# Two-layer graph network: the factor scores of layer 1's loop on GpSimd instead of VectorE

## The chip, the cores and the metric

The kernel runs on one core of a Trainium2 chip. The metric is device time in microseconds (us) of one execution; several executions are taken and their median is given. Engines: TensorE (PE, its weight loads PEld), VectorE (DVE), ScalarE (ACT), GpSimd (POOL) and the DMA queues.

## The reference

Two layers over 2708 nodes with 128 features and a 0/1 adjacency matrix. Layer 0 is a normalised diffusion plus a cosine-similarity attention, with a residual and a layer norm. The change is in layer 1:

```python
XW = jnp.matmul(X, W)
s_col = jnp.matmul(XW, a[0, :f])
s_row = jnp.matmul(XW, a[0, f:])
Z1 = jax.nn.leaky_relu(s_row[:, None] + s_col[None, :], negative_slope=0.01)
den = jnp.exp(Z1)
num = jnp.matmul(A, den)
att = jnp.where(num != 0, den / jnp.where(num != 0, num, 1.0), 0.0)
H = jnp.matmul(A, jnp.matmul(att, XW))
x = _layernorm(x + H)
```

## The kernel before, in words

Nodes are cut into 22 tiles of 128 (T = 22, the last one short). For layer 1 the kernel first ranks all nodes by s_col and by s_row. With columns in that order, the leaky relu of a tile of 128 columns has its kink only in a short window of rows; every row outside the window is on one known side, where exp(s_row + s_col) is a product of two factors. So `num` for a tile jt is a matrix product over few rows: one or two sets of 128 gathered rows of the adjacency (WN = 2; `win` holds the kind: 0 for one set, 1 for two, 2 for a window too wide for this), and a table of sums for all the rest. `FIRST = 4` separates tiles whose window data come early from the others.

The left operands of these products ("factors") lie in `den_w`, `den_h`: for each tile three slots of 128x128 fp32, in a ring of two tiles (DS = 3). A slot is filled in three steps. First the scores: for the window sets q = 0 and, in kind 1, q = 1, `max(s_col + Rw, slope part + r01w)` in the form (column block + per-partition value) max (per-partition value), and for the table slot (column block + e_bias) min e_cap. Second ScalarE's exponential (`den_exp_small`, L718 and L720, one 128x256 instruction, and one more 128x128 in kind 1). Third the low halves: the rest of the fp32 value over its upper bfloat16, computed for the window sets on GpSimd (`halves`, L492 in kind 1, L496 in kind 0) and for the table slot on VectorE (`sums_half`, L1261). TensorE waits for both (`s_denb`) before it sums tile jt.

The loop of layer 1 runs over v = 0..65, three steps v (two blocks of 452 columns each) to a tile. TensorE: `num(v)` (gathered rows L1708, table L1716), then `xw_product(v - 3)` (L1768). ScalarE: two logarithms of the sums (L731), `attention_exp(v - 1)` (L709), and at v = 3(jt-1) + 1 `den_exp_small(jt)`. VectorE: `attention_scores(v)` (L1322), `attention_low(v - 1)` (L1329), at the first step of a tile `small_scores(jt + 1, True)` (L1228 for the window sets, L1247 for the table), at the second `sums_half(jt + 1)`. GpSimd runs by tiles, in order: `fetch_rows(jt)` (two indirect DMAs, L463), `halves(jt - 1)`, `fetch_xw(jt + 4)` (one indirect DMA, L454, up to jt = 17), `split_xw(jt)` (a cast L472 and a subtraction L474 of 128x128).

Each engine carries out its own list in order; semaphores order the engines. `s_num` counts finished sums (6 to a tile), `s_denz` scores (3 to a tile), `s_dene` exponentials, `s_denb` low halves. There is a second form of the loop for inputs with wide windows (`general`); the inputs here take the first.

Of the kernel before, what the change touches and what calls it, by code (L numbers as in the profile page):

```python
# [7 lines left out]
T = 22  # L8
# [19 lines left out]
DS = WN + 1  # L28
# [11 lines left out]
ALU = mybir.AluOpType  # L40
# [42 lines left out]
def rows_of(t):  # L83
    return P if t < T - 1 else LAST


def adj_resnorm2_kernel(nc, x, adjT, alpha, beta, W, a, rowk, out):
    with ExitStack() as ctx:
        def sb(name, shape, dt=F32):
            return ctx.enter_context(nc.sbuf_tensor(name, shape, dt))  # L90

        def sem(name):
            return ctx.enter_context(nc.semaphore(name))
# [27 lines left out]
        tab_part, is_u, e_cap, slot0, no_node = (kc[:, q:q + 1] for q in range(5))  # L121
        own_tile = kc[:, 5:5 + T]
        win = sb("win", [1, 2 * T + 1], I32)
# [34 lines left out]
        e_bias = FR[:, 3356:3356 + T]  # L158
        Rw = FR[:, 3378:3378 + WN * T].rearrange("p (q t) -> p q t", q=WN)
        r01w = FR[:, 3422:3422 + WN * T].rearrange("p (q t) -> p q t", q=WN)  # L160
# [23 lines left out]
        den_w = R1[:, DEN0:DEN0 + NDEN * P].rearrange("p (t j) -> p t j", t=NDEN)  # L184
# [7 lines left out]
        cb3 = cb.rearrange("p (t j) -> p t j", t=T)  # L192
# [55 lines left out]
        s_cball, s_cbc, s_mask, s_count, s_win, s_tabs, s_pick, s_ebias, s_tabh, s_tab = (  # L248
            sem(n) for n in ("s_cball", "s_cbc", "s_mask", "s_count", "s_win", "s_tabs", "s_pick", "s_ebias",
                             "s_tabh", "s_tab"))  # L250
        s_denz, s_dene, s_denb = sem("s_denz"), sem("s_dene"), sem("s_denb")
        s_num, s_ln, s_sub, s_att1, s_alo, s_y, s_xws = (
            sem(n) for n in ("s_num", "s_ln", "s_sub", "s_att1", "s_alo", "s_y", "s_xws"))
# [14 lines left out]
        V, S, G, TE = nc.vector, nc.scalar, nc.gpsimd, nc.tensor  # L268
# [47 lines left out]
        FIRST = 4  # L316
# [37 lines left out]
        def _(eng):  # L354
            gp = Waiting(eng)
# [50 lines left out]
            met = gp.covered()  # L406
# [15 lines left out]
            for it in range(T):  # L422
                m, s = rows_of(it), it % 2
# [29 lines left out]
            def fetch_xw(t):  # L453
                G.indirect_dma_start(out=XWs[:, t, :], out_offset=None, in_=XWd,  # L454
                                     in_offset=bass.IndirectOffsetOnAxis(ap=idx[:, 1, t:t + 1], axis=0)
                                     ).then_inc(s_AT[t], 16)

            def fetch_rows(jt):
                gp.wait_ge(s_idxw, 1 if jt < FIRST else 2)
                if jt >= 3:  # L460
                    gp.wait_ge(s_num, 6 * (jt - 2))
                for q in range(WN):
                    G.indirect_dma_start(out=AW2[:, jt % 3, q, :], out_offset=None, in_=ATd,  # L463
                                         in_offset=bass.IndirectOffsetOnAxis(ap=idxw[:, q, jt:jt + 1], axis=0)
                                         ).then_inc(s_AW[jt % 3], 16)

            def split_xw(t):

                gp.wait_ge(s_AT[t], 32)
                if t >= 4:  # L470
                    gp.wait_ge(s_y, 3 * (t - 3))
                G.tensor_copy(XW2[:, t % 4, 1, :], XWs[:, t, :]).then_inc(s_xws, 1)  # L472
                gp.wait_ge(s_xws, 2 * t + 1)
                G.tensor_tensor(XW2[:, t % 4, 0, :], XWs[:, t, :], XW2[:, t % 4, 1, :], ALU.subtract).then_inc(s_xws, 1)  # L474
# [10 lines left out]
            def halves(jt):  # L485

                s = T + jt % 2 * DS
                kind = eng.value_load(win[0:1, jt:jt + 1], min_val=0, max_val=2)
                gp.wait_ge(s_dene, jt + 1)
                met = gp.covered()  # L490
                with eng.If(kind == 1):
                    G.tensor_tensor(den_h[:, s + 1:s + DS, :, 0], den_w[:, s + 1:s + DS, :], den_h[:, s + 1:s + DS, :, 1],  # L492
                                    ALU.subtract).then_inc(s_denb, 1)
                gp.only(met)
                with eng.Else():
                    G.tensor_tensor(den_h[:, s + 1, :, 0], den_w[:, s + 1, :], den_h[:, s + 1, :, 1], ALU.subtract).then_inc(s_denb, 1)  # L496
                gp.only(met)

            def layer1(general):

                for jt in range(2, T):
                    fetch_rows(jt)
                    if not general:
                        halves(jt - 1)
                    if jt + 4 < T:
                        fetch_xw(jt + 4)
                    split_xw(jt)
                if not general:
                    halves(T - 1)

# [2 lines left out]
            met = gp.covered()  # L513
# [255 lines left out]
        def _(eng):  # L769
# [166 lines left out]
            met, steps = dv.covered(), own.n  # L936
# [145 lines left out]
            for it in range(T):  # L1082
                m, s = rows_of(it), it % 2
# [141 lines left out]
            def score(jt, q):  # L1225

                s = T + jt % 2 * DS
                return V.tensor_scalar(den_w[:, s + 1 + q, :], cb3[:, jt, :], Rw[:, q, jt:jt + 1], r01w[:, q, jt:jt + 1],  # L1228
                                       ALU.add, ALU.max)

            def small_scores(jt, usual):

                s = T + jt % 2 * DS
                if jt >= 2:
                    dv.wait_ge(s_num, 6 * (jt - 1))
                dv.wait_ge(s_pick, 2 if jt < FIRST else 4)
                if usual:
                    kinds[jt] = eng.value_load(win[0:1, jt:jt + 1], min_val=0, max_val=2)
                    met = dv.covered()
                    with eng.If(kinds[jt] == 1):  # L1240
                        score(jt, 1)
                    dv.only(met)
                    score(jt, 0).then_inc(s_denz, 2)
                else:
                    for q in range(WN):
                        score(jt, q).then_inc(s_denz, 1)
                V.tensor_scalar(den_w[:, s, :], cb3[:, jt, :], e_bias[:, jt:jt + 1], e_cap, ALU.add, ALU.min).then_inc(s_denz, 1)  # L1247
# [16 lines left out]
            def den_scores(jt):  # L1264

                dv.wait_ge(s_win, WIN)
                dv.wait_ge(s_pick, 2 if jt < FIRST else 4)
                dv.wait_ge(s_ebias, 1)
                dv.wait_ge(s_cbc, 6)
                where["wide"] = eng.value_load(win[0:1, T + jt:T + jt + 1], min_val=0, max_val=1)  # L1270
                met = dv.covered()
                with eng.If(where["wide"] == 0):
                    small_scores(jt, False)
                dv.only(met)
# [39 lines left out]
            def attention_scores(v):  # L1314

                c0, w = wide_of(v)
                dv.wait_ge(s_negc, 1)
                dv.wait_ge(s_rbm, 6)
                dv.wait_ge(s_ln, 2 * v + 2)
                if v >= NZ:  # L1320
                    dv.wait_ge(s_y, v - NZ + 1)
                V.scalar_tensor_tensor(z_of(v), rb[:, c0:c0 + w], negc[:, v // 3:v // 3 + 1], tL[v % 2][:, 0:w],  # L1322
                                       ALU.max, ALU.subtract).then_inc(s_sub, 1)

            def attention_low(v):

                high, lower = halves_of(v)
                dv.wait_ge(s_att1, v + 1)
                V.tensor_tensor(lower, z_of(v), high, ALU.subtract).then_inc(s_alo, 1)  # L1329

            def layer1(general):

                for v in range(NV):
                    jt, cp = v // 3, v % 3
                    attention_scores(v)
                    if v:
                        attention_low(v - 1)
                    if jt + 1 < T:
                        if general:
                            if cp == 0:  # L1340
                                den_scores(jt + 1)
                            if cp == 1:
                                den_halves(jt + 1)
                            if cp == 2:
                                den_all(jt + 1)
                        else:
                            if cp == 0:
                                small_scores(jt + 1, True)
                            if cp == 1:
                                sums_half(jt + 1)  # L1350
                    if v == 0:
                        table(3)
                        window_rows(FIRST, T, 4)
                    if v == 1:
                        table(4)
                        table(5)
                attention_low(NV - 1)
# [3 lines left out]
            met, steps = dv.covered(), own.n  # L1361
# [499 lines left out]
```

## Time and profile before

| | |
|---|---|
| median of 3 runs | 676.37 us (675.48 to 677.48) |
| profiled execution | 675.03 us |
| its span in the profile | 673.3 us |
| busy over the span: PE, DVE, ACT, POOL | 569.4, 544.2, 352.8, 435.7 us |
| granted TensorE clock, mean | 0.944 |

The span is what the rows below cover; 1.7 us of the profiled execution lie around it. Times are in us from the start of the span unless marked ns. Busy shares are averages over stages that differ much. An instruction's line (L1708) is that of the kernel's text. Layer 1's loop runs from about 393 to 591 us.

### The profile page before, as it was taken

Reading aid. Unit: us, or ns where it says so; the run is one execution under the profiler, and the core shown is the slowest. Engines: PE = TensorE matmul, PEld = TensorE weight load, DVE = VectorE, ACT = ScalarE, POOL = GpSimd, SP = SyncE. Lnnn points to the kernel's source line nnn. Section 1 sums busy time; section 2 is a strip of 40 time slices with the busy share of each in tenths; the row PEclk is TensorE's granted clock in tenths of the full one; section 3 lists DMA queues with packets and bytes.
Section 4 is the critical chain, followed back from the end, with each engine's and each line's share of the span. In section 5 each row is a group of like instructions: output and inputs, shape, how many; then the busy total and the mean of one; then the engine's idle time right before and its main releaser. Section 6 shows DMA issues by size and latency. Waiting matters only on the chain.

```text
span 673.3 us, 11277 instructions
## 1 busy us (share of the span) xinstructions
PE 569.4 (85%) x4123; PEld 348.4 (52%) x4123; DVE 544.2 (81%) x965; ACT 352.8 (52%) x568; POOL 435.7 (65%) x448
## 2 busy tenths in 40 slices
PE   0489999999998679999718988898989999949993
PEld 0245555455453368888617644344445444427883
DVE  1679999999999973678888766899898999985442
ACT  2334544444443542579986226787777788811000
POOL 5849999999998933556305043687786788203663
PEclk9999999999999589999757989999999999988997
DMA  9999891000000000000000041323242333000000
GB/s 148 101 108 108 108 380 51 0 1 1 1 1 1 5 1 17 18 24 17 18 1 21 5 125 46 77 82 103 63 110 72 91 95 98 21 5 13 29 28 18
DMA packets 17797, 37.21 MB, mean 55 GB/s; under 512 B 2570, under 2 KB 8222, under 8 KB 17726
## 3 DMA queue, kind: packets, MB, share of 16 engines
q0 software_dynamic: 7392, 24.32, 20.2%
q1 hardware_dynamic: 10334, 11.98, 5.4%
q8 instruction: 39, 0.64, 0.4%
q14 instruction: 32, 0.26, 0.1%
HBM read 48.72 MB, written 10.45 MB: 88 GB/s over the span
## 4 chain that ended last, share of the span: by engine, by line
PE 35%; POOL 25%; DVE 22%; issue 7%; ACT 7%; DMA 2%; DVEq 0%; POOLq 0%; ACTq 0%; SPq 0%
POOL R L401 23%; PE PSALL L1809 8%; PE PSALL L1708 5%; PE PSALL L1515 5%; DVE ring L1329 4%; DVE ring L1322 4%; ACT AW L629 4%; PE PSALL L1637 3%; PE PSALL L1768 3%; PE PSALL L1441 2%; DVE FR L1329 2%; DVE FR L1322 1%; PE PSALL L1716 1%; PE PSALL L1538 1%; DMA X<-in_x 1%
## 5 line engine op out<-in xcount | busy, mean ns | idle before, releaser
L401 POOL TENSOR_TENSOR R<-R,ring 128x452 f32<-128x452 f32 (+1 forms) x126 | 174.9, 1424 | 5.5 <-ACT ring L560 5.5
L560 ACT ACTIVATE ring<-ring,sm 128x452 f32<-128x452 f32 (+1 forms) x132 | 85.0, 669 | 106.0 <-DVE ring L908 105.9
L913 DVE TENSOR_TENSOR AW<-ring 128x452 bf16<-128x452 f32 (+1 forms) x88 | 105.2, 1196 | 0.0
L1441 PE MATMUL PSALL<-XN 128*128 128x452 f16 (+2 forms) x396 | 99.0, 361 | 5.5 <-issue 4.2
L1708 PE MATMUL PSALL<-AW,R 128*128 128x452 fp8e4 (+1 forms) x348 | 78.4, 357 | 16.6 <-DVE R L1261 10.3
L908 DVE TENSOR_TENSOR ring<-PSALL,AT 128x452 f32<-128x452 f32 (+1 forms) x132 | 78.6, 616 | 3.3 <-PE PSALL L1441 2.9
L463 POOL DMA_INDIRECT AW<-ATd,FR x44 | 55.3, 1258 | 31.7 <-DVE FR L1212 17.1
L1768 PE MATMUL PSALL<-ring,XW 128*128 128x452 bf16 (+1 forms) x300 | 67.7, 360 | 0.9 <-DVE ring L1329 0.9
L1441 PEld LDWEIGHTS PSALL<-XN 128*128 128x128 f16 (+1 forms) x396 | 37.6, 98 | 58.1 <-issue 25.4
L1329 DVE TENSOR_TENSOR ring<-ring 128x904 bf16<-128x904 f32 (+1 forms) x50 | 62.6, 1252 | 0.0
L1515 PE MATMUL PSALL<-R,AT 128*128 128x256 f16 x484 | 61.6, 287 | 0.0
L1708 PEld LDWEIGHTS PSALL<-AW,R 128*128 128x128 bf16 x348 | 32.4, 98 | 56.1 <-DVE R L1261 17.2
L1809 PE MATMUL PSALL<-R,AT 128*128 128x256 f16 x484 | 55.1, 279 | 2.0 <-DVE R L1395 2.0
L1496 PE MATMUL PSALL<-ring,AO 128*128 128x452 bf16 (+1 forms) x176 | 50.3, 367 | 4.4 <-DVE AW L913 3.2
L1515 PEld LDWEIGHTS PSALL<-R,AT 128*128 128x128 fp8e4 x484 | 48.8, 103 | 7.8
L1809 PEld LDWEIGHTS PSALL<-R,AT 128*128 128x128 fp8e4 x484 | 48.3, 100 | 8.6 <-DVE R L1395 2.1
L709 ACT ACTIVATE ring<-ring,st 128x904 f32<-128x904 f32 (+1 forms) x50 | 52.3, 1046 | 0.3 <-DVE ring L1322 0.3
L731 ACT ACTIVATE R<-PSALL,sm 128x452 f32<-128x452 f32 x66 | 38.5, 635 | 24.0 <-PE PSALL L1716 20.7
L731 ACT ACTIVATE TL<-PSALL,sm 128x452 f32<-128x452 f32 x66 | 38.5, 635 | 19.7 <-PE PSALL L1716 17.5
L1768 PEld LDWEIGHTS PSALL<-ring,XW 128*128 128x128 bf16 x300 | 28.6, 96 | 31.6 <-DVE ring L1329 2.0
L1322 DVE SCALAR_TENSOR_TENSOR ring<-R,st,TL 128x904 f32<-128x904 f32 (+1 forms) x33 | 38.4, 1162 | 7.2 <-ACT TL L731 6.7
L629 ACT ACTIVATE AW<-R 128x128 bf16<-128x128 bf16 (+21 forms) x30 | 42.7, 1422 | 2.2 <-DVE R L1008 0.4
(262 smaller groups left out, 1035.3 us busy)
## 6 DMA issues: line engine op xcount, KB each, us to landing
AT<-in_adjT POOLq DMA_DIRECT2D x22, 338.5 KB, 32.6
ATd<-AT SPq DMA_DIRECT2D x2, 3723.5 KB, 16.6
XWd<-ring SPq DMA_DIRECT2D x11, 128.0 KB, 1.8
out<-ring SPq DMA_DIRECT2D x21, 64.0 KB, 1.5
AW<-ATd,FR POOLq DMA_INDIRECT x44
X<-XWd,idx POOLq DMA_INDIRECT x22, 2.6
Wt<-in_W SPq DMA_DIRECT2D x1, 64.0 KB, 11.0
X<-in_x SPq DMA_DIRECT2D x1, 0.5 KB, 7.8
```

The lines of the kernel that those rows point to most:

```text
L401: i = G.tensor_tensor(ES_, ES_, z, ALU.add)
L560: S.activation(z, z, ACT.Exp, scale=bcol[0:rows, :]).then_inc(s_exp, 1)
L731: S.activation(tL[v % 2][:, q * RW:(q + 1) * RW], PSALL[:, 6 + q, 0:RW], ACT.Ln, bias=tiny).then_inc(s_ln, 1)
L908: V.tensor_tensor(z, PSALL[0:rows, b, 0:w], A_, ALU.mult).then_inc(s_z, 1)
L913: V.tensor_tensor(Fl[q % 6][0:rows, 0:w], ring[0:rows, q % 6, 0:w], upper(q, rows, w), ALU.subtract).then_inc(s_low, 1)
L1322: V.scalar_tensor_tensor(z_of(v), rb[:, c0:c0 + w], negc[:, v // 3:v // 3 + 1], tL[v % 2][:, 0:w], ALU.max, ALU.subtract).then_inc(s_sub, 1)
L1329: V.tensor_tensor(lower, z_of(v), high, ALU.subtract).then_inc(s_alo, 1)
L1441: m = TE.matmul(PSALL[0:rows, b, 0:w], lh[:, jt * P:jt * P + rows], rh[:, c0:c0 + w], start=(k == 0), stop=(k == 2))
L1515: ins = TE.matmul(PSALL[:, it % 4, 0:2 * D], AT[:, jt, it * P:(it + 1) * P], xp[:, jt, :, :].rearrange("p c d -> p (c d)"), start=(jt == 0 ...
L1708: TE.matmul(PSALL[:, b, 0:w], den_h[:, s + 1 + q, :, part], AW[:, jt % 3, q, c0:c0 + w], start=(q == 0 and part == 1), stop=False)
L1768: m = TE.matmul(PSALL[:, c, 0:CH[c][1]], XW2[:, jt % 4, part, :], att[:, part_of], start=(jt == 0 and k == 0), stop=(jt == T - 1 and k == 2))
L1809: return TE.matmul(PSALL[:, out_bank[it], 0:2 * D], AT[:, jt, it * P:(it + 1) * P], xpY[:, jt, :, :].rearrange("p c d -> p (c d)"), start= ...
```

## The change

From tile 2 on, in the form of the loop taken here, the scores are computed by GpSimd, at the end of its iteration jt, after `split_xw(jt)`. VectorE still computes those of tiles 0 and 1. The waits, the semaphore counts and the arithmetic are those of before. A register load and a branch on the tile's kind move along.

```diff
+            def score(jt, q):
+                s = T + jt % 2 * DS
+                return G.tensor_scalar(den_w[:, s + 1 + q, :], cb3[:, jt, :], Rw[:, q, jt:jt + 1], r01w[:, q, jt:jt + 1],
+                                       ALU.add, ALU.max)
+
+            def small_scores(jt):
+                s = T + jt % 2 * DS
+                gp.wait_ge(s_denz, 3 * jt)
+                gp.wait_ge(s_num, 6 * (jt - 1))
+                gp.wait_ge(s_pick, 2 if jt < FIRST else 4)
+                kind = eng.value_load(win[0:1, jt:jt + 1], min_val=0, max_val=2)
+                met = gp.covered()
+                with eng.If(kind == 1):
+                    score(jt, 1)
+                gp.only(met)
+                score(jt, 0).then_inc(s_denz, 2)
+                G.tensor_scalar(den_w[:, s, :], cb3[:, jt, :], e_bias[:, jt:jt + 1], e_cap, ALU.add, ALU.min).then_inc(s_denz, 1)
+
             def layer1(general):
...
                     split_xw(jt)
+                    if not general:
+                        small_scores(jt)
                 if not general:
                     halves(T - 1)
...
                         else:
-                            if cp == 0:
-                                small_scores(jt + 1, True)
+                            if v == 0:
+                                small_scores(1, True)
                             if cp == 1:
                                 sums_half(jt + 1)
```

## Rows read from the trace of the kernel before

**Rows 1.** The page: engine, busy us, share of the span, instructions.

```profile
PE 569.4 (85%) x4123; PEld 348.4 (52%) x4123; DVE 544.2 (81%) x965; ACT 352.8 (52%) x568; POOL 435.7 (65%) x448
```

**Rows 2.** Timeline of VectorE: start us, us, line, what, idle before.

```profile
547.43 0.36 DVE L1228 TENSOR_SCALAR R<-XN,FR 128x128 f32<-128x128 f32 x1
547.68 0.36 DVE L1247 TENSOR_SCALAR R<-XN,FR,kc 128x128 f32<-128x128 f32 x1
547.94 1.18 DVE L1322 SCALAR_TENSOR_TENSOR ring<-R,st,TL 128x904 f32<-128x904 f32 x1
549.01 1.25 DVE L1329 TENSOR_TENSOR ring<-ring 128x904 bf16<-128x904 f32 x1
550.29 0.36 DVE L1261 TENSOR_TENSOR R<-R 32x128 bf16<-32x128 f32 x1
```

**Rows 3.** Timeline of TensorE, the window sums at the start of steps.

```profile
464.30 1.70 PE L1708 MATMUL PSALL<-AW,R 128*128 128x452 fp8e4 x8 [1.10 <-DVE R L1261]
...
467.42 1.69 PE L1708 MATMUL PSALL<-AW,R 128*128 128x452 fp8e4 x8
...
542.85 0.94 PE L1708 MATMUL PSALL<-AW,R 128*128 128x452 fp8e4 x4 [0.65 <-DVE R L1261]
...
545.21 0.93 PE L1708 MATMUL PSALL<-AW,R 128*128 128x452 fp8e4 x4
...
550.70 0.94 PE L1708 MATMUL PSALL<-AW,R 128*128 128x452 fp8e4 x4 [0.65 <-DVE R L1261]
```

**Rows 4.** Timeline of ScalarE in the same tile.

```profile
546.37 1.17 ACT L731 ACTIVATE TL<-PSALL,sm 128x452 f32<-128x452 f32 x2 [0.25 <-PE PSALL L1716]
547.42 1.05 ACT L709 ACTIVATE ring<-ring,st 128x904 f32<-128x904 f32 x1
548.36 0.41 ACT L720 ACTIVATE R<-R 128x256 f32<-128x256 f32 x1
```

**Rows 5.** Timeline of GpSimd: one whole period, and a later halves.

```profile
541.18 1.46 POOL L496 TENSOR_TENSOR R<-R 128x128 bf16<-128x128 f32 x1 [0.40 <-ACT R L720]
542.79 0.97 POOL L454 DMA_INDIRECT X<-XWd,idx  x1
543.76 0.37 POOL L472 CAST XW<-X 128x128 bf16<-128x128 f32 x1
544.22 1.25 POOL L474 TENSOR_TENSOR XW<-X,XW 128x128 bf16<-128x128 f32 x1
545.62 1.66 POOL L463 DMA_INDIRECT AW<-ATd,FR  x1 [0.15 <-issue]
547.59 1.02 POOL L463 DMA_INDIRECT AW<-ATd,FR  x1 [0.30 <-issue]
549.03 1.46 POOL L496 TENSOR_TENSOR R<-R 128x128 bf16<-128x128 f32 x1 [0.42 <-ACT R L720]
...
556.88 1.43 POOL L496 TENSOR_TENSOR R<-R 128x128 bf16<-128x128 f32 x1 [0.71 <-ACT R L720]
```

**Rows 6.** Groups of GpSimd's instructions by form: count, busy us, mean ns, idle before.

```profile
L437 POOL TENSOR_SCALAR AO<-ring,ln 128x128 f32<-128x128 f32 x21 | 17.1, 813 | 7.4 <-DVE AO L991 5.2
...
L492 POOL TENSOR_TENSOR R<-R 128x256 bf16<-128x256 f32 x6 | 7.8, 1295 | 12.1 <-ACT R L720 12.1
```

**Rows 7.** Timeline before the loop: a VectorE instruction and a GpSimd one beside it.

```profile
391.86 0.62 DVE L1182 SCALAR_TENSOR_TENSOR R<-R,PSALL 128x448 f32<-128x448 f32 x1
392.09 0.43 POOL L474 TENSOR_TENSOR XW<-X,XW 128x128 bf16<-128x128 f32 x1
```

**Rows 8.** Timeline of GpSimd: halves of tiles 6 to 9.

```profile
454.30 1.48 POOL L496 TENSOR_TENSOR R<-R 128x128 bf16<-128x128 f32 x1 [0.40 <-ACT R L720]
...
462.35 1.74 POOL L492 TENSOR_TENSOR R<-R 128x256 bf16<-128x256 f32 x1 [0.59 <-ACT R L720]
...
472.12 1.15 POOL L492 TENSOR_TENSOR R<-R 128x256 bf16<-128x256 f32 x1 [2.71 <-ACT R L720]
...
481.33 1.06 POOL L496 TENSOR_TENSOR R<-R 128x128 bf16<-128x128 f32 x1 [2.59 <-ACT R L720]
```

## The prediction

> **What bounds the kernel now.** I read the page first, for the busy shares [rows 1]: over the whole span TensorE is at 85%, VectorE at 81%, GpSimd at 65%. That is an average over stages and settles nothing about the loop that is changed, so the rest was read from the timelines of the loop (393 to 591 us of the span), engine by engine, and then the grouped instructions of GpSimd for prices.
>
> The loop has 22 tiles, each with three steps v. There are two sorts: a tile with two sets of gathered rows ("kind 1": 6 tiles, as the count of halves at L492 tells [rows 6]), and one with a single set ("kind 0": the others). In kind 1, TensorE repeats its step every 3.12 us (464.30 to 467.42) without idling [rows 3], so a tile takes 9.3 us and TensorE bounds it. In kind 0 the step is 2.36 us (542.85 to 545.21), three of them 7.05 us, but the tiles start 7.85 us apart (542.85 to 550.70): at each tile start TensorE idles 0.65 us, put down to VectorE's sums_half (L1261) [rows 3]. VectorE works without a gap there: score, table score, attention_scores, attention_low, sums_half follow each other from 547.43 to 550.65 [rows 2].
>
> But sums_half is only one of two conditions of that tile start. The other is GpSimd's halves (L496): it ran 549.03 to 550.49, and TensorE started at 550.70. sums_half ended at 550.65. The two are 0.16 us apart [rows 2, 3, 5]. And GpSimd is not an idle engine in this loop: from 541.18 to 549.03 it runs halves 1.46, fetch_xw 0.97, the cast 0.37, the subtraction 1.25, and two row gathers 1.66 and 1.02 us, with gaps of 0.15, 0, 0.09, 0.15, 0.31 between them; the only gap that is a wait is the last, 0.42 us for ScalarE's exponential, which ended at 548.77 [rows 4, 5]. So of a period of 7.85 us it has 7.43 us of work and issue. Over the whole span it looks 65% busy; here it is full.
>
> **The change part by part.** *Removed from VectorE:* from tile 2 on, two instructions a tile in kind 0 (three in kind 1), with a register load and a branch. They start 0.25 and 0.26 us apart (547.43, 547.68, 547.94) [rows 2], so 0.51 us a tile goes, 0.76 in kind 1. In kind 0 they lie on the chain attention_scores, attention_low, scores, attention_scores, attention_low, sums_half, TensorE. If nothing else held, 14 kind-0 tiles would give 7 us. What is late next: TensorE start (542.85), its second step (545.21), the logarithms of the second (546.37), attention_exp (547.42), the exponential of the factors (548.36 to 548.77), 0.26 us, halves (to 550.49), 0.21 us, TensorE start [rows 3, 4, 5]. This loop holds no VectorE work and takes 7.85 us less the 0.16 us of slack, 7.69 us. So the removal is worth at most some 0.16 us a kind-0 tile, about 2 us in all, while halves costs what it does.
>
> *Added to GpSimd:* the same two (three) instructions on 128x128 fp32 with two per-partition operands, after split_xw(jt) and ahead of fetch_rows(jt+1) and halves(jt). The nearest row is of that very form, the layer norm's tensor_scalar: 813 ns on GpSimd, 21 times, in a stage where VectorE mostly leaves it alone [rows 6]. VectorE takes 0.25 us for it. In this loop GpSimd also pays for its neighbour: the subtraction of split_xw takes 0.43 us (392.09) beside a VectorE instruction that reads one operand from PSUM (L1182), and 1.25 us beside the loop's VectorE work [rows 5, 7], and ends just after VectorE's current instruction does. That reads as waiting for the end of a two-input VectorE instruction. The bounds of one score are then 0.81 us and 0.81 + 0.82 = 1.63 us. I take 0.8 for the first and 1.2 for the second, 1.1 for the third of a kind-1 tile: between the ends, nearer to the low one, since VectorE will idle part of each period once GpSimd is late.
>
> The Trainium skill (Advanced Engine Details and Errata, section on GpSimd) says the Pool engine shares a read and a write interface with VectorE and conflicts with VectorE instructions that have two SBUF inputs; the 0.43 against 1.25 us agrees [rows 5, 7].
>
> *Work of a GpSimd period afterwards*, kind 0, with fetch_xw: the present 7.43, plus 0.3 for the issue before halves, plus 0.1 of issue and 0.8 + 1.2 for the scores, is 9.8 us. Against it stands relief: with halves as the last condition of the tile start, VectorE has caught up and idles for the first 2 us after it, which is where fetch_xw, the cast and the subtraction run. The subtraction then takes 0.43 to 0.5 instead of 1.25, which takes off 0.75: 9.1 us. GpSimd's queue is in order and none of its waits comes later than its own work (s_num for the scores is met when the tile before has been summed, already so; the gather behind them waits for the same count), so the period of the loop becomes this sum. What is queued behind the scores: the row gathers (needed a whole tile later, 9 us, so hidden) and halves(jt), for which TensorE waits. ScalarE's exponential stands at 5.5 us after the tile start (548.36 against 542.85), the scores would be ready at about 4 to 5, so it is not late; what is late is halves behind the gathers.
>
> *The sum over tiles*, by the start of halves:
> - Six periods of kind 0 with two scores (halves of tiles 5, 6, 10, 15, 16, 17): 9.1 against 7.85 [rows 5], +1.25 each, +7.5.
> - Two periods in which TensorE has a kind-0 tile but three scores are computed (tiles 7, 11): 10.1 against 8.05 (454.30 to 462.35) [rows 8], +2.0 each, +4.0.
> - Three with three scores and a kind-1 tile on TensorE (8, 12, 13): about 10.0 against 9.77 (462.35 to 472.12) [rows 8], +0.3 each, +0.9. Two with two scores there (9, 14): 9.1 against 9.21 (472.12 to 481.33) [rows 8], hidden: 0.
> - Three without fetch_xw (18 to 20): 9.1 less 0.97 and its gap 0.15, and 0.2 more for the second gather, 8.2 against 7.85 (549.03 to 556.88) [rows 5], +0.4 each, +1.2.
> - Tiles 2 to 4 are held by the start of the stage; three scores for tile 3 push halves(3) by some 0.7. +0.7. Tile 21 has no gather behind its scores: -0.1, the slack above.
> Together +14.2 us. The profiled execution took 675.03 us, of which the span is 673.3; it becomes 689.2. The median of the runs is 676.37, 1.3 above it: 690.5, and I say 690.
>
> **Rivals.**
> 1. *GpSimd becomes the bound* (the forecast): 690, and 680 to 703 on its own range. For it: the full queue and the 0.81 us row [rows 5, 6]. Its low end has both scores at 0.81 and the gathers at 1.0 each: 9.1 - 0.4 - 0.65 = 8.05 in a period, +0.2 for six, +0.8 for two (8.86 against 8.05) and the 0.7 of the start: +3.5, 680. Its high end has 1.6 for each score and no relief: 11.0, which over the same list is some +45; I hold this unlikely, as a later GpSimd leaves VectorE idle, and cut at a period of 9.9, 0.8 more in 16 tiles: 703.
> 2. *VectorE's relief wins* (faster): GpSimd's instructions shrink, because VectorE has fewer of its own and idles: subtraction 0.43, gathers 1.0, halves 1.0, scores 0.81: 7.4 us, under the 7.69 of the chain through ScalarE. Then each kind-0 tile gains 0.15 and about 2 to 3 us come back: 674. It decides when the period's GpSimd work is below 7.69, so when the scores and all relief together cost less than 0.26 us more than now. Against it: VectorE's long instructions still fill 6.9 us of a period, so relief for all at once is hardly possible.
> 3. *GpSimd's scores are cheap*: some 0.35 us each. Then the sum is 7.43 + 0.4 + 0.7 - 0.4 = 8.1 us, +0.25 in six, +0.4 in two and nothing else: 677 to 680. Against it: 813 ns in 21 instances of the same form [rows 6].
> The Trainium skill (GPSIMD Engine Reference, Engine selection) has one-input elementwise work on GpSimd at roughly line rate, which would make it this rival; the 813 ns row speaks against it, the same page's general advice to leave elementwise work to VectorE speaks for the first.
> 4. *Contention in full* (each score 1.5 us and more, the subtraction still 1.25): over 703, toward 710. VectorE would have to stay dense although it waits for TensorE.
> 5. *Nothing moves*: GpSimd's lateness and VectorE's saving cancel within the measurement: 675 to 678.
>
> **How the numbers follow.** About 0.3% (2.0 us) is what a measurement of this kernel can tell from no change. Forecast 0.77; full contention 0.08; cheap scores 0.05 (two thirds of it slower by over 0.3%); nothing moves 0.03; relief wins 0.07. Slower: 0.77 + 0.08 + 0.03 = 0.88; same: 0.03 + 0.02 = 0.05; faster 0.07. The range is 680 to 703, leaving out the faster cases and full contention.
>
> **What would show it.** In the changed kernel GpSimd's gap before halves carries no wait for ScalarE in kind-0 tiles, it is busy over 90% of the loop, and TensorE's idle time at tile starts is put down to halves (L496), not L1261. The scores take 0.8 to 1.2 us each. VectorE shows gaps of 1 to 2 us a tile, in front of attention_scores. The subtraction of split_xw falls to about 0.5 us. Kind-0 tiles with fetch_xw take about 9.1 us, kind-1 tiles stay near 9.3 to 10. The stages before 393 us and after the loop keep their length. I am wrong if the scores cost under 0.5 us, if the gathers shrink to 1 us throughout, or if ScalarE's exponential still comes last.

## The result and the profile after

The changed kernel takes 716.16 us (median of 4 runs, 714.05 to 718.15) against 675.92 us for the kernel before in the same session: ratio 1.060, 95% interval 1.057 to 1.063. It is slower, as forecast, but by 40 us and not by 14, and outside the stated range of 680 to 703.

The page of the changed kernel, the line that answers to [rows 1]:

```profile
PE 582.8 (81%) x4123; PEld 353.2 (49%) x4123; DVE 536.5 (75%) x919; ACT 352.8 (49%) x568; POOL 496.6 (69%) x494
```

GpSimd has 61 us more work, VectorE 8 us less. The same page's chain that ended last names GpSimd as the largest part, 40% of the span.

```profile
POOL 40%; PE 26%; issue 12%; DVE 12%; ACT 7%; DMA 1%; POOLq 1%; ACTq 0%; DVEq 0%; SPq 0%
```

Timeline of GpSimd after, one whole kind-0 period, against [rows 5]:

```profile
567.20 0.64 POOL L496 TENSOR_TENSOR R<-R 128x128 bf16<-128x128 f32 x1
567.99 1.73 POOL L454 DMA_INDIRECT X<-XWd,idx  x1
569.72 0.30 POOL L472 CAST XW<-X 128x128 bf16<-128x128 f32 x1
570.11 0.43 POOL L474 TENSOR_TENSOR XW<-X,XW 128x128 bf16<-128x128 f32 x1
570.93 2.25 POOL L502 TENSOR_SCALAR R<-XN,FR 128x128 f32<-128x128 f32 x1 [0.40 <-issue]
573.19 2.29 POOL L517 TENSOR_SCALAR R<-XN,FR,kc 128x128 f32<-128x128 f32 x1
575.64 1.04 POOL L463 DMA_INDIRECT AW<-ATd,FR  x1 [0.16 <-issue]
576.99 0.96 POOL L463 DMA_INDIRECT AW<-ATd,FR  x1 [0.31 <-issue]
577.98 0.62 POOL L496 TENSOR_TENSOR R<-R 128x128 bf16<-128x128 f32 x1
```

No gap in it is a wait. The period is 10.78 us (567.20 to 577.98) where it was 7.85. TensorE and ScalarE in the same tile, against [rows 3, 4]:

```profile
567.89 0.94 PE L1730 MATMUL PSALL<-AW,R 128*128 128x452 fp8e4 x4 [3.59 <-POOL R L496]
...
578.65 0.94 PE L1730 MATMUL PSALL<-AW,R 128*128 128x452 fp8e4 x4 [3.56 <-POOL R L496]
```

```profile
564.92 0.42 ACT L742 ACTIVATE R<-R 128x256 f32<-128x256 f32 x1 [2.19 <-POOL R L517]
```

TensorE idles 3.6 us at the start of these tiles, and the releaser is no longer sums_half but halves, L496. ScalarE's exponential now waits 2.2 us for the scores, which the prediction had excluded. GpSimd in turn waits for that exponential only before the first and the last halves of the loop and in tiles 8 and 12, where TensorE has a kind-1 tile (1.48 and 1.41 us):

```profile
490.17 1.15 POOL L492 TENSOR_TENSOR R<-R 128x256 bf16<-128x256 f32 x1 [1.48 <-ACT R L742]
```

The groups of GpSimd's instructions in the loop after give the price of a score: table L517, window L502.

```profile
L517 POOL TENSOR_SCALAR R<-XN,FR,kc 128x128 f32<-128x128 f32 x20 | 41.1, 2056 | 0.0
L502 POOL TENSOR_SCALAR R<-XN,FR 128x128 f32<-128x128 f32 x26 | 36.8, 1417 | 11.0 <-issue 11.0
```

The scores spread from 0.8 to 6.6 us. What sets an instruction's length is seen by laying VectorE's timeline beside it. First the score that began at 573.19 and ended at 575.48, then the first table score of the loop:

```profile
572.61 1.18 DVE L1344 SCALAR_TENSOR_TENSOR FR<-R,st 128x904 f32<-128x904 f32 x1
573.71 1.23 DVE L1351 TENSOR_TENSOR ring<-ring 128x904 bf16<-128x904 f32 x1
```

```profile
414.98 0.82 POOL L502 TENSOR_SCALAR R<-XN,FR 128x128 f32<-128x128 f32 x1 [4.67 <-issue]
415.80 6.57 POOL L517 TENSOR_SCALAR R<-XN,FR,kc 128x128 f32<-128x128 f32 x1
```

```profile
415.11 1.25 DVE L1344 SCALAR_TENSOR_TENSOR FR<-R,st 128x900 f32<-128x900 f32 x1 [3.18 <-ACT R L753]
...
420.64 1.25 DVE L1351 TENSOR_TENSOR ring<-ring 128x904 bf16<-128x904 f32 x1
```

VectorE's pair ended at 574.94, the score 0.54 us later. Six of VectorE's long instructions, without a gap between them, ended at 421.89; the table score of tile 2 ended 0.48 us after that, after 6.57 us. It is so throughout the loop: 21 scores of over 1.7 us stand by themselves in the timeline, and each ended 0.48 to 0.56 us after one of VectorE's long instructions did; the others that stand alone took 0.8 us, but for one of 1.33.

Over the loop, taken from the first halves to the last (405.88 to 580.32 before, 407.36 to 622.16 after), the length went from 174.4 to 214.8 us, +40.4. That is nearly the whole loss of 42.2 us between the two spans; 1.5 us more lie ahead of the loop and 0.4 behind it, within what runs differ by. TensorE's granted clock was 1.00 over this stretch before and is 0.94 on average after. In the kind-0 tiles that does not show in the length: the period from 457.32, at a mean of 0.68, takes 10.20 us, and the one shown above, at 1.00, takes 10.78. In the kind-1 tiles 8 and 12 it does count. After an idle time of 5.09 us the clock was 0.50 (1.2 of 2.4 GHz), and eight window sums took 3.20 us where they take 1.70 in [rows 3]:

```profile
480.54 3.20 PE L1730 MATMUL PSALL<-AW,R 128*128 128x452 fp8e4 x8 [5.09 <-POOL R L492]
```

The logarithms and the exponential behind these sums came late by it, which is GpSimd's wait at 490.17. In the two tiles together this is worth at most the 2.9 us that GpSimd waits there.

### The profile page after: what moved, and what is told of

The parts are those of the page before. It is cut to its first block, busy times and chain, and to the rows that moved or that the text cites. A ratio compares the mean times of both kernels' runs of the same rounds, so it can differ in the third digit from the quotient of the medians.

```text
span 715.5 us, 11295 instructions
## 1 busy us (share of the span) xinstructions
PE 582.8 (81%) x4123; PEld 353.2 (49%) x4123; DVE 536.5 (75%) x919; ACT 352.8 (49%) x568; POOL 496.6 (69%) x494
## 4 chain that ended last, share of the span: by engine, by line
POOL 40%; PE 26%; issue 12%; DVE 12%; ACT 7%; DMA 1%; POOLq 1%; ACTq 0%; DVEq 0%; SPq 0%
POOL R L401 21%; PE PSALL L1537 5%; PE PSALL L1730 5%; ACT AW L651 3%; POOL AW L463 3%; PE PSALL L1659 3%; POOL R L517 2%; POOL R L502 2%; PE PSALL L1831 2%; PE PSALL L1790 2%; POOL ring L555 2%; POOL X L454 2%; POOL ln L553 1%; PE PSALL L1463 1%; PE PSALL L1738 1%
## 5 line engine op out<-in xcount | busy, mean ns | idle before, releaser
L1730 PE MATMUL PSALL<-AW,R 128*128 128x452 fp8e4 (+1 forms) x348 | 83.7, 375 | 45.2 <-POOL R L496 25.9
L1790 PE MATMUL PSALL<-ring,XW 128*128 128x452 bf16 (+1 forms) x300 | 71.2, 374 | 0.9 <-DVE ring L1351 0.9
L463 POOL DMA_INDIRECT AW<-ATd,FR x44 | 51.5, 1170 | 28.6 <-DVE FR L1234 17.7
L454 POOL DMA_INDIRECT X<-XWd,idx x22 | 32.9, 1498 | 26.4 <-DVE idx L1148 22.4
```

Of the source, the lines that this page charges most:

```text
L1730: TE.matmul(PSALL[:, b, 0:w], den_h[:, s + 1 + q, :, part], AW[:, jt % 3, q, c0:c0 + w], start=(q == 0 and part == 1), stop=False)
L1790: m = TE.matmul(PSALL[:, c, 0:CH[c][1]], XW2[:, jt % 4, part, :], att[:, part_of], start=(jt == 0 and k == 0), stop=(jt == T - 1 and k == 2))
```

## The experiments

Theories. *Occupancy and port*: a tile takes what GpSimd's list takes, and a score's price is set by VectorE's instructions with two SBUF inputs, which it must sit out. *Exponential*: the scores come late to ScalarE, whose exponential holds the logarithms behind it; it is the place of the scores, not their length. *Slow of itself*: a score takes 2 us on GpSimd whatever runs beside it. Ratios are to the kernel before on the same chip.

**VectorE's relief alone.** The kernel before, where nobody computes scores from tile 2 on; ScalarE's exponential reads the column block instead, without waiting for scores:

```diff
-                av.wait_ge(s_denz, 3 * (jt + 1))
+                if jt < 2:
+                    av.wait_ge(s_denz, 3 * (jt + 1))
...
+                two = den_w[:, s:s + 2, :] if jt < 2 else cb3[:, jt, :].unsqueeze(1).broadcast_to([P, 2, P])
...
-                S.activation(den_w[:, s:s + 2, :], den_w[:, s:s + 2, :], ACT.Exp).then_inc(s_dene, 1)
+                S.activation(den_w[:, s:s + 2, :], two, ACT.Exp).then_inc(s_dene, 1)
...
-                            if cp == 0:
-                                small_scores(jt + 1, True)
+                            if v == 0:
+                                small_scores(1, True)
```

> The kernel before without any window or table scores from tile 2 on: ScalarE's exponential reads the column block itself, so the values are not the reference's. This is VectorE's relief alone, with nothing added to GpSimd. By the prediction's chain (TensorE, logarithms, exponential, halves on GpSimd) at most 0.16 us a kind-0 tile can be won: 673 to 676 us. If VectorE alone set the pace, 0.5 us in 14 tiles and 0.2 more where it is late: 667 to 670 us.

Measured: 670.29 us, ratio 0.991 (0.989 to 0.993), 6 us off, below the 673 to 676 of the prediction's chain and just above the 667 to 670 of VectorE alone. TensorE's tile starts are 7.45 us apart:

```profile
532.67 0.94 PE L1711 MATMUL PSALL<-AW,R 128*128 128x452 fp8e4 x4 [0.30 <-DVE R L1264]
...
540.12 0.94 PE L1711 MATMUL PSALL<-AW,R 128*128 128x452 fp8e4 x4 [0.26 <-DVE R L1264]
```

```profile
538.84 1.06 POOL L496 TENSOR_TENSOR R<-R 128x128 bf16<-128x128 f32 x1 [0.49 <-ACT R L723]
```

The prediction's 0.16 us a tile was too small: halves fell from 1.46 to 1.06 us, so the chain through GpSimd gave way too, and VectorE's sums_half is still what comes last. That halves got shorter because VectorE's long instructions stood elsewhere beside it was not tried. 6 us is what the removal is worth with nothing added to GpSimd.

**GpSimd's part alone.** The kernel before, with GpSimd computing the scores a second time into a buffer (scr) that nobody reads, and incrementing no semaphore:

```diff
+        scr = sb("scr", [P, DS, P])
...
+                G.tensor_scalar(scr[:, 1, :], cb3[:, jt, :], Rw[:, 0, jt:jt + 1], r01w[:, 0, jt:jt + 1], ALU.add, ALU.max)
+                G.tensor_scalar(scr[:, 0, :], cb3[:, jt, :], e_bias[:, jt:jt + 1], e_cap, ALU.add, ALU.min)
...
                     split_xw(jt)
+                    if not general:
+                        small_scores(jt)
```

> The kernel before, VectorE's scores kept, with GpSimd computing the same scores once more into a scratch buffer that nobody reads. Occupancy theory: nearly the changed kernel's time, 708 to 722 us, with scores of 1 to 3 us each on GpSimd. Exponential theory: nobody waits for these scores, so only the queue behind them moves: 676 to 690 us.

Measured: 714.83 us, ratio 1.057 (1.055 to 1.060). That is the changed kernel's time within its spread. Nobody waits for these scores, so the exponential theory is out as the main cause, and nearly the whole loss, 38 of 40 us, comes with the instructions added to GpSimd. In the group rows the copies cost about what the scores do:

```profile
L510 POOL TENSOR_SCALAR scr<-XN,FR,kc 128x128 f32<-128x128 f32 x20 | 38.7, 1933 | 0.0
L509 POOL TENSOR_SCALAR scr<-XN,FR 128x128 f32<-128x128 f32 x20 | 30.8, 1541 | 7.3 <-PE PSALL L1731 4.6 <-issue 2.7
```

**The same instructions earlier in the list.**

```diff
+                    if not general:
+                        small_scores(jt)
                     split_xw(jt)
-                    if not general:
-                        small_scores(jt)
```

> The changed kernel with the scores ahead of split_xw(jt) instead of behind it. GpSimd's work is the same, ScalarE gets the scores about 1.2 us earlier. Occupancy theory: the sum of the list decides, 708 to 722 us (the neighbours on VectorE change). Exponential theory: 700 to 706 us.

Measured: 713.33 us, ratio 1.056 (1.051 to 1.062). As by occupancy: moving the scores ahead changed 3 us.

**Less on GpSimd's list.** All fetch_xw ahead of the loop or in its first iteration:

```diff
-            for t in range(6):
+            for t in range(18):
                 fetch_xw(t)
...
                     fetch_rows(jt)
+                    if jt == 2:
+                        for t in range(18, T):
+                            fetch_xw(t)
                     if not general:
                         halves(jt - 1)
-                    if jt + 4 < T:
-                        fetch_xw(jt + 4)
```

> The changed kernel with every fetch_xw issued ahead of the loop or in its first iteration, so that 16 indirect DMAs of 1.5 us (mean in the changed kernel) leave GpSimd's list in the tiles. Occupancy theory (a tile takes what GpSimd's list takes): a kind-0 tile goes from 10.8 to about 9.2 us, in all 18 to 26 us off, 690 to 698 us. Exponential theory (the tile is long because ScalarE's exponential waits for the scores and holds the logarithms behind it): the scores come 1.6 us earlier, so the wait of 2.2 us falls to 0.6 and the gain is about as large, but GpSimd would then show waits for ScalarE before halves in every tile. If neither holds (the gathers' landing or another engine): under 5 us off.

Measured: 701.49 us, ratio 1.036 (1.031 to 1.041), 15 us off the changed kernel. The sign is that of occupancy; the size falls short of the 18 to 26 us expected. The sign that was given for the exponential theory, a wait for ScalarE before halves in every tile, isn't there: besides the first and the last halves three of them wait (1.0 to 2.6 us). The group of the cast accounts for some 7 us of the rest: without the DMA ahead of it, it grew from 520 ns in the changed kernel to

```profile
L472 POOL CAST XW<-X 128x128 bf16<-128x128 f32 x22 | 18.1, 823 | 0.0
```

**Half of the change.** The kernel before, where only the table score moves to GpSimd, at the end of its iteration; the window scores stay on VectorE, and GpSimd gets no register load and no branch. The first line is GpSimd's, the others VectorE's:

```diff
+                G.tensor_scalar(den_w[:, s, :], cb3[:, jt, :], e_bias[:, jt:jt + 1], e_cap, ALU.add, ALU.min).then_inc(s_denz, 1)
...
-                V.tensor_scalar(den_w[:, s, :], cb3[:, jt, :], e_bias[:, jt:jt + 1], e_cap, ALU.add, ALU.min).then_inc(s_denz, 1)
+                if not usual or jt < 2:
+                    V.tensor_scalar(den_w[:, s, :], cb3[:, jt, :], e_bias[:, jt:jt + 1], e_cap, ALU.add, ALU.min).then_inc(s_denz, 1)
```

> Half of the change: only the table score goes to GpSimd, the window scores stay on VectorE; GpSimd has no register load and no branch for them. Occupancy theory: a kind-0 tile loses one score of 1.4 to 2 us and 0.3 us of issue against the changed kernel's 10.8 us, so about 8.8: 684 to 694 us. If the wait for the first score (its place in the list, not its length) were the cost: 705 to 716 us.

Measured: 689.27 us, ratio 1.017 (1.011 to 1.023), as by occupancy. One instruction of this form a tile on GpSimd costs 13 us in all; the rest of the scores and their issue cost 27 more.

**The port by itself.** A small kernel that computes nothing of the network, its stages as listed:

> Not the network: eight stages in which GpSimd runs 8 instructions on 128x128 fp32, beside VectorE doing (0) nothing, (1) 22 instructions with two SBUF inputs of 904 columns without a wait between them, (2) the same with a wait on the one before each, (3) 22 with one input from PSUM, (4) 22 tensor_scalar with one SBUF input, (7) pairs as in the loop with a wait after each pair; in (5) and (6) the VectorE of (1) beside a subtraction and a cast on GpSimd. Port theory (a GpSimd instruction can't get its operands while two-input VectorE instructions follow each other without a gap): 0.8 us each in (0) and (3), in (1) several times that, down to one or none finished before VectorE ends; in (2) and (7) one per gap, 1.2 and 2.4 us. Theory of a fixed slowdown (each takes some 1.2 us beside any VectorE work): the same in (1), (2), (3), (7).

The rows are those of its one line, each for the window of one stage: count, and duration in ns as min/median/max. In order: VectorE idle; two SBUF inputs, no waits; the same with a wait on each; one input from PSUM; tensor_scalar; pairs with a wait after each pair.

```profile
L105 POOL TENSOR_SCALAR GG<-GS,R,Q x9: 792/796/1722, 7.2 to 13.4; 128x128 f32<-128x128 f32 x9
L105 POOL TENSOR_SCALAR GG<-GS,R,Q x8: 1722/2212/2213, 13.4 to 28.3; 128x128 f32<-128x128 f32 x8
L105 POOL TENSOR_SCALAR GG<-GS,R,Q x8: 1281/1282/1722, 37.5 to 46.8; 128x128 f32<-128x128 f32 x8
L105 POOL TENSOR_SCALAR GG<-GS,R,Q x8: 792/796/805, 64.0 to 69.4; 128x128 f32<-128x128 f32 x8
L105 POOL TENSOR_SCALAR GG<-GS,R,Q x8: 1541/1994/1997, 87.6 to 101.0; 128x128 f32<-128x128 f32 x8
L105 POOL TENSOR_SCALAR GG<-GS,R,Q x8: 2217/2218/2642, 151.1 to 167.0; 128x128 f32<-128x128 f32 x8
```

The instruction takes 0.80 us alone and beside VectorE instructions that read PSUM, 2.21 us beside dense ones with two SBUF inputs (each of those 1.10 us from start to start, so two of them), 1.99 us beside VectorE's tensor_scalar, which has one SBUF input (0.66 us from start to start, so three of them), and 1.28 us when each long VectorE instruction waits for the one before, 1.27 us apart. It is not slow of itself, and the surcharge is no fixed slowdown: it comes in whole VectorE instructions. One expectation failed: dense VectorE work was to hold a score for several times 2.2 us, down to one or none finished before its end; here it never held one through more than two. In pairs with a wait after each pair a score takes one pair, 2.22 us against pairs 2.21 us apart (2.4 had been expected); the dense stage has two instructions as well, so a wait after every second one changed nothing.

**Which forms pay it.** A second small kernel, forms of GpSimd's instruction alone and beside the dense VectorE work:

> Not the network: GpSimd instructions on 128x128 fp32, 8 of each, first alone (even stages) and then beside dense two-input VectorE instructions of 1.10 us (odd stages): tensor_scalar with two constants, with one per-partition operand, with two, tensor_tensor with a per-partition operand spread by its access pattern, tensor_tensor with two full inputs. If the per-partition operands are what is slow and what makes a score sit out two VectorE instructions: 0.3 us alone and 1.1 us beside with constants, 0.8 and 2.2 us with two operands. If the operation or fp32 is: 0.8 and 2.2 us in all tensor_scalar forms.

Rows of windows inside the stages; L86 is the form with two constants, L88 with one per-partition operand, L90 with two, L92 tensor_tensor with a spread per-partition operand. Alone, then beside:

```profile
L86 POOL TENSOR_SCALAR GG<-GS x5: 637/638/638, 7.3 to 9.8; 128x128 f32<-128x128 f32 x5
...
L86 POOL TENSOR_SCALAR GG<-GS x7: 1132/1133/1137, 12.8 to 19.4; 128x128 f32<-128x128 f32 x7
...
L88 POOL TENSOR_SCALAR GG<-GS,R x6: 598/603/604, 35.8 to 38.7; 128x128 f32<-128x128 f32 x6
L88 POOL TENSOR_SCALAR GG<-GS,R x6: 2130/2132/2132, 43.2 to 53.7; 128x128 f32<-128x128 f32 x6
L90 POOL TENSOR_SCALAR GG<-GS,R,Q x7: 784/789/790, 64.0 to 68.6; 128x128 f32<-128x128 f32 x7
L90 POOL TENSOR_SCALAR GG<-GS,R,Q x7: 2211/2212/2213, 71.8 to 85.0; 128x128 f32<-128x128 f32 x7
...
L92 POOL TENSOR_TENSOR GG<-GS,R x7: 397/398/398, 94.2 to 96.3; 128x128 f32<-128x128 f32 x7
L92 POOL TENSOR_TENSOR GG<-GS,R x7: 1250/1250/1255, 97.4 to 104.7; 128x128 f32<-128x128 f32 x7
```

Alone the forms with constants are hardly cheaper (0.64 against 0.79; 0.3 had been expected). Beside VectorE tensor_scalar splits in two: without a per-partition operand one VectorE instruction is sat out, with one or two of them two are. Both forms of tensor_tensor sit out one, that with a spread per-partition operand too (the one with two full inputs: 0.46 us alone, 1.31 beside). It is no matter of length: with one per-partition operand tensor_scalar is the shorter one alone (0.60 against 0.64) and the longer one beside VectorE (2.13 against 1.13).

**The same in the loop.** The changed kernel with constants for the per-partition operands, other values than the reference's:

```diff
-                return G.tensor_scalar(den_w[:, s + 1 + q, :], cb3[:, jt, :], Rw[:, q, jt:jt + 1], r01w[:, q, jt:jt + 1],
+                return G.tensor_scalar(den_w[:, s + 1 + q, :], cb3[:, jt, :], 0.125, -20.0,
                                        ALU.add, ALU.max)
...
-                G.tensor_scalar(den_w[:, s, :], cb3[:, jt, :], e_bias[:, jt:jt + 1], e_cap, ALU.add, ALU.min).then_inc(s_denz, 1)
+                G.tensor_scalar(den_w[:, s, :], cb3[:, jt, :], 0.125, 20.0, ALU.add, ALU.min).then_inc(s_denz, 1)
```

> The changed kernel with two constants in place of the per-partition operands of GpSimd's scores from tile 2 on, so the scores are not the reference's. Everything else, the number of instructions, their size and their place, stays. If the per-partition operands are what makes a score sit out a second VectorE instruction, as in the microbenchmark (2.21 against 1.13 us): the table score falls from 2.06 to 1.1 us, the window score from 1.42 to 0.9, 20 x 0.95 + 26 x 0.5 = 32 us less work on GpSimd, of which other waits take some back: 688 to 698 us. If not, 712 to 718 us.

Measured: 694.95 us, ratio 1.030 (1.024 to 1.036), 21 us off the changed kernel with the number and place of the instructions unchanged. The scores themselves took 31 us less (77.9 to 46.9); that the form with constants is cheaper alone, by 0.15 us in each of 46, makes 7 of it.

```profile
L502 POOL TENSOR_SCALAR R<-XN 128x128 f32<-128x128 f32 x26 | 25.1, 965 | 9.7 <-issue 8.8
L517 POOL TENSOR_SCALAR R<-XN 128x128 f32<-128x128 f32 x20 | 21.8, 1092 | 1.6
```

**Gaps on VectorE.** The changed kernel, where VectorE only waits more, first in attention_scores(v), then in attention_low(v):

```diff
                 dv.wait_ge(s_ln, 2 * v + 2)
+                if v >= 2:
+                    dv.wait_ge(s_alo, v - 1)
...
                 high, lower = halves_of(v)
+                if v + 1 < NV:
+                    dv.wait_ge(s_sub, v + 2)
                 dv.wait_ge(s_att1, v + 1)
```

> The changed kernel with one thing added on VectorE: attention_low(v - 1) waits for attention_scores(v) to be done, and attention_scores(v) for the attention_low ahead of it, so that a short gap stands between any two of its long instructions. It does only more waiting. Port theory: a score on GpSimd falls from 2.1 us (table) and 1.4 us (window) towards the 1.28 us of the microbenchmark's stage with waits, since it no longer sits out two VectorE instructions; the kernel gets faster, 692 to 704 us. Any theory in which GpSimd's instructions are long of themselves, or the loop's order or the exponential is what costs: 716 to 720 us, or slower by VectorE's gaps.

Measured: 702.35 us, ratio 1.040 (1.035 to 1.044): 14 us faster than without the waits. The mean table score fell from 2056 to 1263 ns, close to the small kernel's 1282, and none took 6.57 us:

```profile
L517 POOL TENSOR_SCALAR R<-XN,FR,kc 128x128 f32<-128x128 f32 x20 | 25.3, 1263 | 0.0
```

**The same gaps in the kernel before.**

> The kernel before with the same two waits on VectorE. VectorE loses about 0.05 us at each of six long instructions, 0.3 us a kind-0 tile, which it pays on the chain: +3 to +4 us. GpSimd's subtraction, gathers and halves no longer sit out pairs: halves 1.46 to about 1.1 us, which counts only where GpSimd's halves is the last condition. Port theory with halves co-critical: 672 to 679 us; if VectorE alone set the pace: 680 us.

Measured: 682.42 us, ratio 1.010 (1.006 to 1.013), on the side of VectorE setting the pace (680 us), and past its figure. Halves shrank to 0.45 us (at 544.84), more than expected, yet the tiles grew to 8.2 us: TensorE waited 1.00 us for sums_half (at 546.77). So in the kernel before, VectorE's chain is the condition that counts, and the one through GpSimd stands just beneath it (0.16 us by the prediction's rows).

**Fetching early without the change, and with half of it.**

> The kernel before with fetch_xw issued ahead of the loop. GpSimd's list in a kind-0 tile gets 1.1 us shorter, which was no condition of the tile there except through halves' start, which waits for ScalarE's exponential: 673 to 678 us, no change that can be told.

> Table score on GpSimd, window scores on VectorE, and fetch_xw ahead of the loop. GpSimd's list is 7.43 - 1.1 + 2.0 = 8.3 us less relief of 0.4 to 0.8, so 7.5 to 7.9 in a kind-0 tile, level with the 7.85 of the kernel before: 674 to 682 us. Below 674 would make it a better kernel than both.

Measured: 688.60 us (1.019, 1.015 to 1.024) and 696.40 us (1.033, 1.027 to 1.039); both expectations failed. What was lost by the first of them doesn't lie in the loop: from the first halves to the last it takes 174.0 us (420.25 to 594.27), as the kernel before (174.4). It starts 14 us late. Timeline of the stage ahead of it, in this kernel, and VectorE's row in the other one:

```profile
384.34 0.94 POOL L454 DMA_INDIRECT X<-XWd,idx  x1 [0.30 <-issue]
387.84 0.18 DVE L1019 SCALAR_TENSOR_TENSOR ring<-PSALL,st 128x22 f32<-128x22 f32 x1 [16.91 <-remote]
388.05 0.54 ACT L690 ACTIVATE FR<-PSALL 88x452 f32<-88x452 f32 x1 [15.00 <-remote]
```

```profile
387.05 0.18 DVE L1034 SCALAR_TENSOR_TENSOR ring<-PSALL,st 128x22 f32<-128x22 f32 x1 [16.95 <-remote]
```

VectorE and ScalarE stood still for 16.9 and 15.0 us while GpSimd issued its further gathers (the last at 384.34), and TensorE ran with many short gaps. The kernel with half of the change has the same stall, 16.95 and 14.43 us. The changed kernel with early fetches issues the same gathers and shows none, so its gain stands. What held the engines is not shown by the profile (it puts the waits down to "remote") and was not tried. Half of the change with early fetches takes 180.5 us from halves to halves: still 6 us more than the kernel before. Of the kernels that compute the reference's result none here beats the kernel before.

## Why the prediction was right or wrong

*What bounds the loop before:* right. Both conditions of a tile start, VectorE's and GpSimd's, lie close together, and GpSimd's list is full. The run that removes VectorE's scores alone gains 6 us, the one that adds GpSimd's alone loses 38.

*What the removal is worth:* off. 0.16 us a tile was forecast, 0.40 measured (7.85 to 7.45), since halves itself got shorter. It counts for nothing in the changed kernel: 716.16 with it, 714.83 without.

*The mechanism:* right. GpSimd's list becomes the bound, no wait is in it in kind-0 tiles, TensorE's idle time goes to L496, the subtraction falls to 0.43 us and halves from 1.46 to 0.64. One of its own signs of being wrong did come, though in kind-1 tiles only: in tiles 8 and 12 the exponential came last (1.48 and 1.41 us), behind a TensorE at the lower clock, a term that the sum did not have.

*The step that failed* is the price of a score: "I take 0.8 for the first and 1.2 for the second, 1.1 for the third". Measured in the period shown: 2.25 and 2.29 us, 2.5 us above the 2.0 that were put down. The bound of 1.63 was wrong too: it took the surcharge of the subtraction, 0.82 us, one VectorE instruction, over to a form with per-partition operands, which sits out two (2.21 us in the small kernel), and in the extreme six that follow without a gap (6.57 us), which the small kernel doesn't reproduce. Over the loop the 46 scores took 77.9 us, where this price makes it 46.6 (20 tiles of 0.8 + 1.2, six of 1.1 more): 31 us too little, in a sum that came out 26 us short. The hope that a late GpSimd leaves VectorE idle beside the scores held for what comes first after halves, not for the scores, which fell right onto the pairs. The rest of the period gives 0.9 us of it back, so that 10.78 stands against 9.1: fetch_xw 1.73 instead of 0.97 and the issue ahead of the scores 0.40 instead of 0.1 are 1.06 us more, halves 0.82, the gathers 0.68, the issue before halves 0.3 and the two instructions of split_xw 0.1 less. The high end, "11.0, which over the same list is some +45", was near the truth (10.78, +40.4), though by another sum: 1.6 a score and no relief, where 2.3 a score and much relief were measured. What cut the range at 703 was the argument that a later GpSimd leaves VectorE idle; it did (gaps of 1.35, 1.20 and 0.75 us in this period), but not where the scores ran.

*By tiles*, worked from the starts of halves in both traces: the six kind-0 periods lost 15.8 us (7.5 forecast), the two with three scores 7.4 (4.0), the three and the two under kind-1 tiles 4.4 and 3.3 (0.9 and 0), the three without fetch_xw 3.7 (1.2), tiles 2 to 4 lost 6.7 (0.7), 3.9 of it in the period with the one table score of 6.57 us; tile 21 gained 1.0. The sum is 40.4 against 14.2. (Two slips in the forecast's arithmetic are small: three steps of 2.36 us are 7.08, not 7.05, and 9.1 with a third score of 1.1 is 10.2, not 10.1 or 10.0, which would add 0.8 us.) That kind-1 tiles would hide two scores failed by the same term in tiles 9 and 14: GpSimd's list there came to 10.8 us against TensorE's 9.3, with table scores of 2.52 and 2.27 us. In tiles 8 and 12 the three scores ran beside an idle VectorE and took 0.8 us each; the list came to 9.6 and 9.5 us, under the 10.0 forecast, and the rest is the wait for the exponential.

*"ScalarE's exponential ... is not late":* wrong, it waited 2.2 us in kind-0 tiles; but with the same instructions read by nobody the time is the same, so this wait costs nothing that could be told from the list.

*The rivals.* Full contention had 0.08 and "over 703, toward 710", on the assumption that VectorE would have to stay dense. It came nearest, by its price of a score, and was still too short; its other conditions were not met, since the subtraction fell to 0.43 us in most tiles and VectorE had gaps. The conflict rule that the Trainium skill (Advanced Engine Details and Errata, the section on GpSimd) states was borne out: 2.21 us beside VectorE instructions with two SBUF inputs, 0.80 beside ones that read PSUM. The price comes from the runs. The rule of the Trainium skill that made the cheap-scores rival (GPSIMD Engine Reference, Engine selection, one input at about line rate) did not hold for this form: 0.79 us alone against VectorE's 0.25 us from start to start [rows 2].

## What to carry to other kernels

An engine that looks 65% busy over a span can be full in the one stage where work is to be added: sum its list over one period before moving anything onto it. Price an instruction on GpSimd from a row of the same form beside the same VectorE work; a row from a quiet stage, or the surcharge of another form, is no bound. Where a short GpSimd tensor_scalar had to run beside dense two-input VectorE work here, its length was a multiple of VectorE's instruction, and the form without per-partition operands took half of it.

## What the runs showed of the hardware

- A GpSimd tensor_scalar of 128x128 fp32 with per-partition operands: 0.79 us alone, 2.21 us beside back-to-back VectorE instructions of 1.10 us with two SBUF inputs, 1.99 us beside VectorE tensor_scalar in SBUF (0.66 us apart), 0.80 us beside one that reads PSUM. With constants 0.64 and 1.13 us.
- It can be held through more than two: 6.57 us beside six in a row in the changed kernel, 6.18 us in the one with the table score alone. In the small kernel 22 in a row held none through more than two; what makes the difference is open.
- A wait before each of VectorE's long instructions, a gap of 0.04 us in the small kernel, lets GpSimd in: 2.06 to 1.26 us for the table score, and 14 us off the whole kernel although VectorE only waits more. A wait after every second one does not (2.22 us).
- What VectorE pays, in the small kernels: 1.04 us from start to start with GpSimd idle, 1.10 beside GpSimd's tensor_scalar, 1.21 to 1.27 beside its tensor_tensor.
- Eighteen indirect DMAs in a row instead of six went with a standstill of 14 to 17 us on VectorE and ScalarE in two kernels and not in a third. Why is open.
